# Preparation of a graph kernel rebuilt: histogram layout, step list, row statistics and edge flags

## The reference, cut to what matters

```python
x: (6250, 256) f32;  src, dst: (100000,) int32, sorted by dst
h = maximum(layernorm(x), 0)
# first layer, three hops
out_norm = clip(segment_sum(1, src), 1) ** -0.5
in_norm  = clip(segment_sum(1, dst), 1) ** -0.5
for i in range(3):
    h = h * out_norm[:, None]
    h = segment_sum(h[src], dst) * in_norm[:, None]
    h = h @ W[i] + b[i]          # relu after the first two
x = x + h
# second layer: two graph attention convolutions (softmax over the edges of each dst)
x = x + gat_conv(relu(gat_conv(maximum(layernorm(x), 0), ...)), ...)
```

## Time and profile before

| | |
|---|---|
| median of three executions | 6040.2 us (6039.87 to 6041.69) |
| profiled execution, its own time | 6037.3 us |
| its span | 6035.5 us |
| TensorE, VectorE, ScalarE, GpSimd busy | 66%, 65%, 35%, 69% of the span |
| first gather of the first hop issued | 314.16 us after the span's start |
| first hop ends | 1299 us |

### The profile page before, as it was taken

One profiled execution on the slowest core, in us unless ns is written; L12 is line 12 of the kernel. 1 busy time (PEld: TensorE's weight loads), 2 busy tenths in 40 slices (PEclk: granted clock), 3 DMA queues, 4 the chain that ended last, 5 costly groups with the idle time before them and its releaser, 6 DMA issues.

```text
span 6035.5 us, 108824 instructions
## 1 busy us (share of the span) xinstructions
PE 3982.0 (66%) x15144; PEld 2613.3 (43%) x15144; DVE 3947.5 (65%) x12842; ACT 2129.2 (35%) x6879; POOL 4135.8 (69%) x4386
## 2 busy tenths in 40 slices
PE   2156666676666667666666676888777567777772
PEld 1134444454444444444444454555445445454441
DVE  7655555555555555555555676777777757777777
ACT  3100000020000002000000028888888378888883
POOL 2377777756777775677777417777777467777775
PEclk9877787787777778777777787888888878888886
DMA  1233333333333333333333424444444234444444
GB/s 57 60 96 106 106 106 106 106 91 107 106 106 106 106 106 95 106 106 106 106 106 105 122 72 112 110 111 110 109 110 113 78 107 110 110 110 110 110 109 143
DMA packets 311188, 627.31 MB, mean 104 GB/s; under 512 B 87058, under 2 KB 181726, under 8 KB 310528
## 3 DMA queue, kind: packets, MB, share of 16 engines
q0 software_dynamic: 192928, 530.18, 31.6%
q1 hardware_dynamic: 117632, 90.16, 5.0%
HBM read 573.50 MB, written 47.33 MB: 103 GB/s over the span
## 4 chain that ended last, share of the span: by engine, by line
PE 31%; DMA 19%; DVE 19%; POOL 14%; issue 12%; DVEq 3%; ACT 2%; SPq 1%; POOLq 0%
PE main L844 19%; DMA ring<-conv_tab,csrc 15%; POOL ring L589 7%; DVE acc L1152 6%; PE main L970 6%; POOL ring L599 4%; DMA ring<-attn_tab,sidx 3%; PE main L862 3%; DVEq L1152 2%; POOL oh L566 1%; DVE ring L1451 1%; PE pso L889 1%; DVE ring L1025 1%; POOL ring L624 1%; DVE ad L1345 1%
## 5 line engine op out<-in xcount | busy, mean ns | idle before, releaser
L589 POOL DMA_INDIRECT ring<-conv_tab,csrc x2346 | 2221.1, 947 | 731.0 <-issue 466.3
L1152 DVE TENSOR_TENSOR acc<-acc,main 128x257 f32 (+1 forms) x4160 | 1767.6, 425 | 1383.1 <-PE main L844 988.8
L844 PE MATMUL main<-ring,oh 128*128 x4992 | 1920.1, 544 | 1096.7 <-SPq L424 861.0
L844 PEld LDWEIGHTS main<-ring,oh 128*128 128x128 f32 x4992 | 1248.9, 271 | 1767.4 <-issue 1548.4
L599 POOL DMA_INDIRECT ring<-attn_tab,sidx x1664 | 1600.0, 962 | 526.9 <-issue 378.5
L970 PE MATMUL main<-ring,oh 128*128 128x264 f32 x3328 | 1223.2, 479 | 112.3 <-ACT ring L748 96.8
L748 ACT ACTIVATE ring<-ring 128x64 f32<-128x64 f32 x3328 | 912.9, 341 | 0.0
L1144 DVE TENSOR_SCALAR oh<-iota,dloc 128x128 f32<-128x128 f32 x2505 | 771.2, 308 | 198.8 <-issue 97.1
L662 ACT ACTIVATE nb<-acc 128x256 f32<-128x256 f32 x147 | 57.9, 404 | 2079.2 <-DVE acc L1152 1980.2
L970 PEld LDWEIGHTS main<-ring,oh 128*128 128x128 f32 x3328 | 598.3, 221 | 266.7 <-DVE ring L1451 185.0
L726 ACT ACTIVATE oh<-iota,dloc 128x128 f32<-128x128 f32 x1752 | 555.4, 392 | 18.8 <-DMA attn_tab<-oh 18.8
(11 more groups left out here) (210 smaller groups left out, 2805.2 us busy)
## 6 DMA issues: line engine op xcount, KB each, us to landing
ring<-conv_tab,csrc POOLq DMA_INDIRECT x2346, 2.8
ring<-attn_tab,sidx POOLq DMA_INDIRECT x1664
attn_tab<-oh SPq DMA_DIRECT2D x14, 910.0 KB, 4.2
conv_tab<-oh SPq DMA_DIRECT2D x14, 896.0 KB, 4.0
ring<-attn_tab SPq DMA_DIRECT2D x14, 896.0 KB, 4.9
flag_room<-start_rows SPq DMA_DIRECT2D x424, 8.0 KB
flag_room<-end_rows SPq DMA_DIRECT2D x424, 8.0 KB
conv_tab<-acc SPq DMA_DIRECT2D x7, 896.0 KB, 14.6
```

The source lines that it names most:

```text
L589: pool.indirect_dma_start(ring3[:, c % U, 0:C], None, conv_tab[k], bass.IndirectOffsetOnAxis(ap=csrc[:, c:c + 1], axis=0)).then_inc(gather ...
L844: nc.tensor.matmul(main[s % 4][:, 0:C + 1], oh[:, (s % OHR) * P:(s % OHR + 1) * P], ring[:, bass.ds(at, C + 1)], start=True, stop=True).th ...
L1152: nc.vector.tensor_tensor(a, a, main[k][:, 0:width], ALU.add).then_inc(added, 1)
```

## The change

- src is read directly as 125 rows of 800 (`lin`), and dst directly by chunk (`drow_c`), both before the loads of x; the padded tables are written between parts of x and are needed only by the step gathers. `csrc` comes straight from src, behind the loads of x. GpSimd first fills the pads and two wide iotas (2560 and 980 columns).
- The histogram's one-hots are laid out with the 20 columns of a batch innermost: VectorE compares runs of 20 bf16 that lie side by side, and TensorE reads one-hots at a stride of 20 elements. There are 40 batches of 20 pairs.
- The step list comes from the first and the last edge of each chunk: two comparisons of 7 x 49 columns, two products with ones, two reductions. The 49 Sign passes go.
- Mean and variance of x are taken by ScalarE with two accumulating passes a tile, beside the histogram. The scales are worked out four double batches before the histogram's end.
- The 14 step gathers are ordered dst first; only dst is needed before the hop.
- VectorE clears `acc` in seven memsets after the table is stored; GpSimd no longer does, and its first gather no longer waits for the clearing.
- Keys, flags, `sidx` and `endt` are worked out in steps 48 to 156 of hop 1; their seven DMAs go out on ScalarE's queue.

```diff
-HB = 17
-NH = EC // (2 * HB)
+HB = 20
+LP = 125
+LC = E // LP
+NH = LC // (2 * HB)
...
-        oh_lo = ring[:, o_lo:o_hi].bitcast(BF16).rearrange("p (b k n) -> p b k n", b=2, n=P)
-        oh_hi = ring[:, o_hi:o_hi + HB * NT].bitcast(BF16).rearrange("p (b k n) -> p b k n", b=2, n=NT)
+        oh_lo = ring[:, o_lo:o_hi].bitcast(BF16).rearrange("p (b n k) -> p b n k", b=2, k=HB)
+        oh_hi = ring[:, o_hi:o_hi + HB * NT].bitcast(BF16).rearrange("p (b n k) -> p b n k", b=2, k=HB)
...
-            sp.dma_start(src_pad.rearrange("a b -> (a b)")[0:E].rearrange("(k f) -> k f", k=16),
-                         src.rearrange("(k f) -> k f", k=16)).then_inc(edges_in, 16)
-            sp.dma_start(dst_pad.rearrange("a b -> (a b)")[0:E].rearrange("(k f) -> k f", k=16),
-                         dst.rearrange("(k f) -> k f", k=16)).then_inc(edges_in, 16)
+            sp.wait_ge(pads_set, 1)
+            sp.dma_start(lin[0:LP, :], src.rearrange("(p f) -> p f", p=LP)).then_inc(lin_in, 16)
+            sp.wait_ge(pads_set, 3)
+            def chunk_rows(to, of, sem):
+                a, r = (KB - 1) * P, E // P
+                sp.dma_start(to[:, 0:KB - 1, :], of[0:a * P].rearrange("(b p e) -> p b e", p=P, e=P)).then_inc(sem, 16)
+                sp.dma_start(to[0:r - a, KB - 1, :], of[a * P:r * P].rearrange("(p e) -> p e", e=P)).then_inc(sem, 16)
+                sp.dma_start(to[r - a:r - a + 1, KB - 1, 0:E - r * P], of[r * P:E].rearrange("(p e) -> p e", p=1)
+                             ).then_inc(sem, 16)
+            chunk_rows(drow_c, dst, dst_rows_in)
             for q in range(7):
                 sp.dma_start(xa[:, q * TB:min((q + 1) * TB, NFULL), :],
                              x[q * TB * P:min((q + 1) * TB, NFULL) * P, :].rearrange("(t p) c -> p t c", p=P)
                              ).then_inc(x_in, 16)
-            sp.wait_ge(pads_set, 2)
+                if q == 1:
+                    sp.dma_start(src_pad.rearrange("a b -> (a b)")[0:E].rearrange("(k f) -> k f", k=16),
+                                 src.rearrange("(k f) -> k f", k=16)).then_inc(edges_in, 16)
+                    sp.dma_start(dst_pad.rearrange("a b -> (a b)")[0:E].rearrange("(k f) -> k f", k=16),
+                                 dst.rearrange("(k f) -> k f", k=16)).then_inc(edges_in, 16)
...
-            sp.wait_ge(edges_in, 32)
-            sp.wait_ge(pads_out, 64)
-            sp.dma_start(lin, src_pad.rearrange("a b -> (a b)").rearrange("(p f) -> p f", p=P)).then_inc(lin_in, 16)
-            sp.wait_ge(lin_in, 16)
-            sp.dma_start(dlin, dst_pad.rearrange("a b -> (a b)").rearrange("(p f) -> p f", p=P)).then_inc(lin_in, 16)
-            sp.dma_start(b3(csrc[:, 0:(KB - 1) * P]), src_pad[0:(KB - 1) * P, :].rearrange("(b p) e -> p b e", p=P)
-                         ).then_inc(chunk_rows_in, 16)
-            sp.dma_start(csrc[0:KL, (KB - 1) * P:KB * P], src_pad[(KB - 1) * P:EC, :]).then_inc(chunk_rows_in, 16)
...
+            nc.gpsimd.memset(lin[96:P, :], OUTSIDE).then_inc(pads_set, 1)
+            pool.wait_ge(pads_set, 1)
+            nc.gpsimd.memset(drow_c[:, KB - 1, :], OUTSIDE).then_inc(pads_set, 1)
+            pool.wait_ge(pads_set, 2)
+            nc.gpsimd.memset(csrc[:, (KB - 1) * P:KB * P], 0).then_inc(pads_set, 1)
+            link(nc.gpsimd.iota(iota_lo, pattern=[[1, P], [0, HB]], base=0, channel_multiplier=0,
+                                allow_small_or_imprecise_dtypes=True))
+            nc.gpsimd.iota(iota_hi, pattern=[[1, NT], [0, HB]], base=0, channel_multiplier=0,
+                           allow_small_or_imprecise_dtypes=True).then_inc(hist_iotas, 1)
             nc.gpsimd.memset(padi, OUTSIDE).then_inc(pads_set, 1)
-            link(nc.gpsimd.memset(strayf, -5.0))
+            nc.gpsimd.memset(strayf, -5.0).then_inc(pads_set, 1)
...
-            pool.wait_ge(lin_in, 32)
-            for b in range(SB):
-                for row, tab in ((srow, src_pad), (drow, dst_pad)):
+            pool.wait_ge(edges_in, 32)
+            pool.wait_ge(pads_out, 64)
+            for row, tab, sem_in in ((drow, dst_pad, dst_steps_in), (srow, src_pad, src_steps_in)):
+                for b in range(SB):
                     pool.indirect_dma_start(b3(row)[:, b, :], None, tab,
                                             bass.IndirectOffsetOnAxis(ap=ci[:, b:b + 1], axis=0)
-                                            ).then_inc(rows_in, 16)
-            def clear_first():
-                pool.wait_ge(table_stored, 16 * NI)
-                for i in range(0, NT):
-                    pool.nop(nofuse=True)
-                    nc.gpsimd.tensor_copy(acc[:, bass.ds(i * AW, AW)], zrow[:, :]).then_inc(acc_clear, 1)
+                                            ).then_inc(sem_in, 16)
...
-            clear_first()
             pool.wait_ge(steps_ready, 1)
             link(nc.gpsimd.memset(xr[:, NFULL, :], 0.0))
-            nc.gpsimd.memset(ring3[:, 0:U, ONES_COL:ONES_COL + 1], 1.0).then_inc(steps_ready, 1)
+            link(nc.gpsimd.memset(ring3[:, 0:U, ONES_COL:ONES_COL + 1], 1.0))
+            nc.gpsimd.memset(zrow[:, 0:1], 0.0).then_inc(steps_ready, 1)
...
-            act.wait_ge(dlin_ready, 1)
+            act.wait_ge(x_in, 16 * 8)
             for t in range(NT):
-                link(nc.scalar.activation(sgn, dlin_f, ACT.Sign, scale=-1.0, bias=thr[:, t:t + 1],
-                                          accum_out=cnt[:, t:t + 1]))
-            nc.scalar.copy(t1[:, 0:1], cnt[:, 0:1]).then_inc(counts_ready, 1)
+                link(nc.scalar.activation(scrap, xa[:, t, :], ACT.Copy, scale=1.0 / C, accum_out=stat3[:, t, 0:1]))
+                link(nc.scalar.activation(scrap, xa[:, t, :], ACT.Square, scale=-1.0,
+                                          bias=stat3[:, t, 0:1], accum_out=stat3[:, t, 1:2]))
+            nc.scalar.copy(t1[:, 2:3], stat3[:, 0, 0:1]).then_inc(ln_stats, 1)
...
+            act.wait_ge(keys_ready, 1)
+            nc.scalar.dma_start(keys[0:1, 1:1 + SX * P].rearrange("o (b p e) -> (o p) b e", p=P, e=P),
+                                key[:, :, 1:P + 1]).then_inc(key_out, 16)
+            with nc.allow_non_contiguous_dma(reason="one element of each step"):
+                act.wait_ge(key_out, 16)
+                kv = keys[0:1, 0:SX * P].rearrange("o (b p e) -> (o p) b e", p=P, e=P)
+                nc.scalar.dma_start(key[:, :, 0:1], kv[:, :, 0:1]).then_inc(key_edge, 16)
+                kn = keys[0:1, 2:SX * P + 2].rearrange("o (b p e) -> (o p) b e", p=P, e=P)
+                nc.scalar.dma_start(key[:, :, P + 1:P + 2], kn[:, :, P - 1:P]).then_inc(key_edge, 16)
+                act.wait_ge(flags_ready, 1)
+                nc.scalar.dma_start(start_rows.rearrange("(b p) e -> p b e", p=P), b3(sfr)).then_inc(flags_out, 16)
+                nc.scalar.dma_start(end_rows.rearrange("(b p) e -> p b e", p=P), b3(efr)).then_inc(flags_out, 16)
+                nc.scalar.dma_start(start_any.rearrange("o (b p) -> (o p) b", p=P), sany).then_inc(flags_out, 16)
+                nc.scalar.dma_start(end_any.rearrange("o (b p) -> (o p) b", p=P), eany).then_inc(flags_out, 16)
+                act.wait_ge(flags_out, 64)
...
-                            mm = nc.tensor.matmul(psad[:, 0:NT], oh_lo[:, b, j, :], oh_hi[:, b, j, :], start=False,
+                            mm = nc.tensor.matmul(psad[:, 0:NT], oh_lo[:, b, :, j], oh_hi[:, b, :, j], start=False,
...
+            hist(0, 2)
             pe.wait_ge(counts_ready, 1)
-            nc.tensor.matmul(main[0][:, 0:NT], ones[:, :], cnt, start=True, stop=True).then_inc(counts_sum, 1)
-            hist(NH // 2, NH)
+            nc.tensor.matmul(main[0][:, 0:KB * NT], ones[:, :], cmpf, start=True, stop=True)
+            nc.tensor.matmul(main[1][:, 0:KB * NT], ones[:, :], cmpl, start=True, stop=True).then_inc(counts_sum, 1)
+            hist(2, NH)
...
+            def late_rows(s):
+                for table, w, first, n in ((srowf, 2, SROW_AT + 2, SB), (efr, 3, EROW_AT + 2, 2 * SB)):
+                    b = (s - first) // 4
+                    if 0 <= b < SB and (s - first) % 4 == 0:
+                        pe.wait_ge(rowsf_ready, w)
+                        pe.wait_ge(rowsT_read, n + b - 1)
+                        nc.tensor.transpose(pso[b % 2][:, 0:P], b3(table)[:, b, :], ident[:, :]).then_inc(rowsT_done, 1)
...
-                        for to, of, n in ((oh_lo, lo_b, P), (oh_hi, hi_b, NT)):
+                        for to, of, of_iota, n in ((oh_lo, lo_b, iota_lo, P), (oh_hi, hi_b, iota_hi, NT)):
                             mm = nc.vector.tensor_tensor(
                                 to[:, c, :, :],
-                                of[:, bass.ds((2 * i + c) * HB, HB)].rearrange("p (k o) -> p k o", o=1)
-                                .to_broadcast([P, HB, n]),
-                                iota_b[:, 0:n].rearrange("p (o n) -> p o n", o=1).to_broadcast([P, HB, n]),
-                                ALU.is_equal)
```

(54 more changed lines are left out.)

189 lines of the change are left out of this document (76 added, 113 removed).

## The result

The changed kernel takes 5874.4 us (median of 4 runs, 5870.1 to 5878.5) where the kernel before takes 6040.9 us beside it (4 runs, 6039.9 to 6042.0): ratio 0.9724, with a 95% interval of 0.9707 to 0.9741. The profiled execution took 5874.1 us, of which the span is 5872.2 us, and lies on the median.

The account below looks back on a forecast made before the run. The preparation, running on one engine at a time, was taken to delay hop 1's first gather, after which GpSimd sets the pace: 6037.3 - 179.7 + 3.3 = 5860.9 us, with the median 2.9 us above, so 5864; range 5848 to 5945.

Parts of the forecast that it names:

- The start: Beginning of the preparation: the histogram's first comparison at 9.7 us instead of 33.8, behind two wide iotas and three memsets.
- The comparisons: VectorE's one-hot comparisons in the histogram: two columns at a time, 1.4 and 0.6 us, 1.97 us a batch.
- The rival with one column at a time: Histogram comparisons on VectorE stay at one column a time: 3.83 us a batch, 5934 us in all; chance 7%.
- The stride: TensorE's histogram operands read at 40 bytes: still 52 ns a pair, not bounding while under 98 ns.
- the rival in which TensorE bounds the histogram: Strided reads make TensorE the histogram's bound: 5900 us at 3 us a batch, 5996 at 5.4; chance 20%.
- ScalarE's statistics: Mean and variance of x beside the histogram: x in at 28 us, 56.5 us for 49 tiles, done at 84.6.
- The step gathers: 14 GpSimd gathers in the preparation: some pass at 80 to 86 us, the rest follow 102; dst landed by 109.
- Hop 1: First hop: VectorE's clearing and flags' work covered by GpSimd's lead; held gathers cost 3.3 us, between 0 and 6.5.
- The rival in which the hop doesn't keep up: Lag of 27 to 40 us in hop 1's first 160 steps makes GpSimd wait: 5881 us; chance 9%.
- No difference after 1120 us: Rest of the kernel, where nothing is changed: any difference after 1120 us would show the forecast wrong.
- One engine at a time: Preparation before the change: VectorE busy nearly throughout both histogram halves, TensorE a quarter, then GpSimd alone clearing for 18 us.
- the rival at 7.5 us a batch: Slower than before: strided TensorE reads in the histogram above 6.6 us a batch; at 7.5, 6078 us; chance 3%.

Follow-up runs that it names:

- the old order: The changed kernel with the histogram's one-hots written and read with 128 or 49 values innermost, still 20 columns a batch: 5934.4 us (one run).
- pairs: The changed kernel with two columns of a batch innermost instead of 20, TensorE reading at a 4-byte stride, and one smaller iota: 5881.0 us, ratio 0.9736.
- packed reads: The changed kernel with TensorE reading the same one-hot bytes as packed columns instead of at a 40-byte stride, counts wrong: 5873.2 us (one run).
- GpSimd's clearing: The changed kernel with GpSimd clearing the sums in 49 copies before its first gather, VectorE's seven memsets out: 5890.1 us (one run).

## Why the prediction was right, and where it was off

The predicted time, 5864 us, is 10.4 us under the median, inside the range. Against the profiled execution's own time (5874.1 against 5860.9) the sum is 13.2 us short: 6.9 us before the first gather, 1.3 us given back in hop 1, and 7.5 us behind it, where the prediction had nothing. Step by step, as the prediction put them:

| step | predicted | measured |
|---|---|---|
| first comparison | 9.7 | 11.4 |
| a batch | 1.97 | 2.12 |
| step list done | 28.8 | 30.6 |
| x in | 28 | 30.4 |
| statistics of a tile; done | 1.15; 84.6 | 1.18; 88.2 |
| scales done | 86.3 | 91.0 |
| out-degree scales done | 105.1 | 111.7 |
| relu done | 129.3 | 135.9 |
| first gather | 134.5 | 141.35 |
| hop 1, longer by | 3.3 | 2.0 |

- **The start** was 1.7 us late: the iota of 2560 columns took 2.91 us instead of 2.4, and the iota of 128 columns that took 0.25 us before took 0.50. It cost nothing at the end, since ScalarE's line decides up to 88 us. (Other executions of the same preparation start at 10.9 to 11.4 us.)
- **The comparisons** are right: 1.49 and 0.66 us. The rival with one column at a time is dead, and the old order shows its price, 3.83 us a batch, which the bound had to the hundredth. The rule of the Trainium skill on performance modes (Vector Engine (DVE) Microarchitecture Reference, Performance modes) is borne out (1.49 us against 2.81 in the old order), with pairs also for an innermost run of only two (1.48).
- **The stride** is the term that was mis-sized. I took 52 ns a pair of load and product and gave 98 ns as the edge; it was 102. That the price lay just past that edge and not far beyond it was luck: the prediction had no row for it. So the rival in which TensorE bounds the histogram is half true: the waits come from both sides, a batch takes 0.14 us more, and what reached the end is the last eight batches with TensorE's last, 1.8 us. What the Trainium skill says without a price (Advanced Engine Details and Errata, Memory Cachelines) has one here: twofold at 40 bytes, nothing at 4.
- **ScalarE's statistics** carried 4.7 of the 6.9 us that the first gather was late: x in 2.4 us later, 0.025 us more a tile (1.2 us for 49), and 1.1 us in the scales, since the square root loads a table (1.28 us), a row I hadn't looked for. The 0.1 us for a bias from memory can't be had from the two rows that the prediction names, but it came out: the passes take 0.42 and 0.51 us. With 1.8 us of the batches, 0.1 of the scales and 0.3 of the store this makes 6.9.
- **The step gathers** did better than forecast: with VectorE pausing in each batch they passed one a batch, 1.5 to 1.9 us each but one of 0.9, and were through at 60 us. The prediction had one standing until VectorE is through with the scales; with packed reads, where VectorE doesn't pause, one did, for 44.8 us.
- **Hop 1**: the clearing is hidden, as the run without it confirms, and GpSimd's waits stay at 0.3 us. Three gathers beside two-input instructions were lengthened, 1.3 us in all above 0.94; the hop grew by 2.0. That six would be held for half of their length was a guess and came out too high. The rival in which the hop doesn't keep up has nothing for it.
- **"No difference after 1120 us"** was wrong in the profile: 7.5 us of the gain at the end of hop 1 (170.8) are gone at the end (163.3). By the medians 4.3 us are (170.8 - 166.5). From first gather to end the kernel before needs 5721.3 us; the old order and packed reads need 5726.7 and 5726.8, GpSimd's clearing 5728.6, the changed kernel 5730.9 and the pairs 5731.8. So all five with the new preparation are longer, and scatter of single executions doesn't obviously explain it. From the last gather of hop 3 to the first of attention it is 214.8 us before and 216.8 to 218.6 in the five, at a granted clock of 0.87 before and 0.84 to 0.87 in them. The cause is open.
- **"One engine at a time"** reads the earlier trace rows too simply: they have ScalarE at 52.36 of the first 79 us and one held gather on GpSimd for the 82 us of the second half. Two slips in the prediction's arithmetic carry nothing: 9.4 - 8.8 is 0.6 us a burst and not 0.65, and the rival at 7.5 us a batch comes to 6080 us by its own formula, not 6078.

The runs put a price on four parts at the first gather: the order of the one-hots 64.6 us, the statistics 28.7, the flags 28.2, the clearing 18.3, of 172.8 in all. The other parts were not undone by runs of their own. The traces show where they lie: the first comparison starts at 11.4 us instead of 33.8, and VectorE no longer stands 16.5 us for the step gathers behind the histogram.

## What to carry to other kernels

After several engines have been set side by side, the one that ends last has often been started last: look at what its first instruction waits for (one count for eight loads; small transfers issued before the last of them is counted) before making the others faster. A layout that pleases one engine can often be had with the smallest innermost run that does it, here two, at no cost to the other. And a queue that issues in order is a place on the critical path: moving a few small transfers from in front of seven stores was worth 28 us, not through their bytes but because the stores could go out while the rows were being made.
